# A linear-attention layer with a Hadamard FFN on one core: 32-wide corner tiles in the inverse, the FFN weight fold moved into the setup, clearings moved ahead, and new step orders

## What is computed

```
qkvz = xn @ w_qkvz.T ;  q, k, v, z per head        (32 heads of 64)
q, k, v = causal conv over 4 tokens, per channel
g = -exp(A_log) * softplus(a + dt_bias) ; beta = sigmoid(b)
q, k = l2norm(q) / 8, l2norm(k)
for t:  S = S * exp(g_t) ; delta = (v_t - k_t S) * beta_t
        S = S + k_t^T delta ; o_t = q_t S
attention = (rmsnorm(o) * norm_weight * sigmoid(z)) @ w_out.T

u = fwht(xn * SU_ug) ; h = silu(u W_gate) * (u W_up)      (1024 wide)
ffn = (fwht(h * SU_dp) @ W_down.T) * Wscale_dp
```

## Time and profile before

| | us |
|---|---|
| median of 3 runs | 921.9 (918.11 to 922.74) |
| the profiled execution, its own time | 921.86 |
| its span | 920.0 |
| TensorE busy | 845.0 (92%) |
| VectorE busy | 703.3 (76%) |
| GpSimd busy | 287.7 (31%) |
| ScalarE busy | 256.0 (28%) |

### The profile page before, as it was taken

The page is one execution under the profiler, slowest core; times in us unless marked ns, Lnnn a source line. Parts: engine busy times, 40 slices in busy tenths (PEclk is TensorE's granted clock), DMA queues, the critical chain, the costliest instruction groups (busy, mean ns, idle before and its releaser), DMA issues.

```text
span 920.0 us, 30578 instructions
## 1 busy us (share of the span) xinstructions
PE 845.0 (92%) x13354; PEld 607.2 (66%) x13354; DVE 703.3 (76%) x1248; ACT 256.0 (28%) x560; POOL 287.7 (31%) x194
## 2 busy tenths in 40 slices
PE   1887499999999999999999999999999999998685
PEld 1533267766767676767676677767777767767574
DVE  5675968888887979788887878797978888795522
ACT  2333114132332314141423223241414132331000
POOL 2019531514124242324142322423231513233110
PEclk9989699999999999999999999999999999999877
DMA  4323031131413131413213141304131231210101
GB/s 124 128 58 81 6 77 36 31 82 30 94 30 83 23 80 37 69 32 64 60 31 82 30 94 24 89 19 77 42 58 44 41 84 30 60 31 14 30 2 46
DMA packets 129157, 49.56 MB, mean 54 GB/s; under 512 B 110977, under 2 KB 120449, under 8 KB 128897
## 3 DMA queue, kind: packets, MB, share of 16 engines
q1 hardware_dynamic: 129024, 47.62, 23.8%
HBM read 39.98 MB, written 7.60 MB: 52 GB/s over the span
## 4 chain that ended last, share of the span: by engine, by line
PE 60%; DVE 17%; SPq 7%; DMA 6%; POOL 5%; issue 3%; ACT 1%; POOLq 0%; DVEq 0%; ACTq 0%
PE bank L581 17%; DVE kq L224 4%; PE bank L645 4%; PE bank L593 3%; PE bank L747 3%; SPq L512 3%; PE bank L662 3%; PE bank L749 3%; PE bank L692 3%; PE bank L602 3%; PE bank L664 3%; PE bank L730 2%; PE bank L668 2%; PE bank L719 2%; PE bank L678 2%
## 5 line engine op out<-in xcount | busy, mean ns | idle before, releaser
L581 PE MATMUL bank<-xnT,wq 128*128 128x512 f32 x512 | 261.8, 636 | 15.8 <-DVE kq L224 15.5
L224 DVE SCALAR_TENSOR_TENSOR kq<-bank,cw,kq 128x510 f32<-128x510 f32 (+2 forms) x288 | 214.6, 745 | 44.9 <-ACT kq L798 37.8
L581 PEld LDWEIGHTS bank<-xnT,wq 128*128 128x128 f32 x512 | 90.7, 195 | 98.1 <-issue 70.3
L948 POOL TENSOR_TENSOR ost<-ost,cst 128x8 f32<-128x8 f32 x32 | 52.3, 1634 | 191.7 <-DVE ost L357 191.7
L798 ACT ACTIVATE kq<-bank,cw 128x512 f32<-128x512 f32 x96 | 65.8, 685 | 143.3 <-PE bank L581 142.5
L944 POOL TENSOR_TENSOR Sd<-St,dec 128x256 f32<-128x256 f32 x32 | 19.9, 621 | 231.7 <-DVE St L345 161.4
L938 POOL TENSOR_TENSOR kqg<-kq,rows 128x1024 f32<-128x1024 f32 x32 | 75.5, 2358 | 39.0 <-DVE kq L224 39.0
L645 PE MATMUL bank<-kq 64*64 64x128 f32 x1024 | 69.0, 274 | 11.6 <-DVE kq L224 8.9
L911 POOL TENSOR_TENSOR kd<-kc,stat 128x512 f32<-128x512 f32 x32 | 33.4, 1042 | 144.1 <-DVE stat L261 144.1
L747 PE MATMUL bank<-wo,oT 128*128 128x256 f32 x256 | 70.6, 389 | 1.6 <-DVE oT L369 1.6
L270 DVE TENSOR_TENSOR ATP<-bank,gb 128x512 f32<-128x512 f32 x64 | 44.1, 689 | 30.4 <-issue 14.3
(11 more groups left out here) (132 smaller groups left out, 1449.1 us busy)
## 6 DMA issues: line engine op xcount, KB each, us to landing
rows<-decay_rows SPq DMA_DIRECT2D x64, 256.0 KB, 4.6
wq<-wqkvz_dram SPq DMA_DIRECT2D x16, 512.0 KB, 3.7
inverse_blocks<-UU SPq DMA_DIRECT2D x16, 256.0 KB, 2.0
woraw<-wout_dram SPq DMA_DIRECT2D x16, 128.0 KB, 2.2
wguT<-wgu_dram SPq DMA_DIRECT2D x8, 256.0 KB, 5.2
base_blocks<-ATP SPq DMA_DIRECT2D x128, 16.0 KB, 2.7
NT<-base_blocks SPq DMA_DIRECT2D x16, 128.0 KB, 2.1
U<-inverse_blocks SPq DMA_DIRECT2D x128, 16.0 KB, 2.0
```

The lines of the kernel that those rows point to most:

```text
L224: nc.vector.scalar_tensor_tensor(out=y[:, :, t:S], in0=p[:, :, 0:S - t], scalar=cw[:, m, i // 2, 3 - t:4 - t], in1=y[:, :, t:S], op0=ALU.m ...
L581: last = nc.tensor.matmul(ring[i % 2][:], wq[:, q, kc, i // 2, :], xnT[:, kc, (i % 2) * 512:(i % 2) * 512 + 512], start=kc == 0, stop=kc = ...
L948: nc.gpsimd.tensor_tensor(ost[:, 2, :], ost[:, 1, :], k("neghalf")[:, 0:B * 2], ALU.pow).then_inc(rms_done, 1)
```

## The change

- **Corner tiles.** hz.1 on TensorE is cut from one 64 x 64 corner for a head to the two 32 x 32 corners on its diagonal (twice the matmuls, 48 columns each). hz.3 loads only the 32 left columns of Q and writes the top 32 rows.
- **Fold in the setup.** `fold` is gone from GpSimd. W_down is loaded early into the memory of `kqg` (`wds`); VectorE multiplies it by wsd (two halves) and does six butterflies of 128 x 1024 in the setup; TensorE's 128-wide part then waits for them, and ScalarE's copy takes in the scale. The two multiplications stand around `var` (L395), one butterfly ahead of each of VectorE's two copies of xnT, four behind `coef`. GpSimd's first `kqg.0` waits for `wd_ready`.
- **Clearings first.** The four memsets stand ahead of the layernorm's power.
- **DMAs.** wsd, ah (4) and nwh (2) are issued by ScalarE ahead of its first squares; SyncE's wait for xnT is gone.
- **Orders.** All five lists are new. They are turned round (other letters), and apart from that these steps move. TensorE: ktr.1 from behind ks.3 to between proj.4 and ks.3; gram.0 from ahead of proj.4 to behind ks.3; proj.6 from ahead of vtr.0 to ahead of proj.7; qsq from ahead of delta.1 to behind it, proj.2 ahead of delta.1. VectorE: vtr.0 from behind gram.1 to behind hz.3.1; inv.1 from behind ks.2 to behind state.1; proj.2 behind ks.2; out.0 ahead of proj.5. ScalarE: qsq, qsum, dec, delta.3 and oload move, inv.2 ahead of proj.5. GpSimd: kd.0 from ahead of gb.0 to behind kqg.1, kd.1 from ahead of sd.2 to behind it, kqg.0 ahead of norm.1. SyncE: load from behind bin to ahead of bout, oload between bout and bin, fload behind uout.

```diff
@@ vector, setup
+                def butterfly(src, dst, h, t):
+                    s4, d4 = (w.rearrange("p (a t h) d -> p a t h d", t=2, h=h) for w in (src, dst))
+                    step(nc.vector.tensor_tensor(d4[:, :, t], s4[:, :, 0], s4[:, :, 1], (ALU.add, ALU.subtract)[t]))
+                def wscaled(i):
+                    step(nc.vector.tensor_tensor(wds[1][:, 4 * i:4 * i + 4], wds[0][:, 4 * i:4 * i + 4], wsd[:].unsqueeze(1).broadcast_to([P, 4, HID]), ALU.mult))
+                dve.wait_ge(wdn_in, 16)
+                dve.wait_ge(wsd_in, 16)
+                wscaled(0)
                 dve.wait_ge(sq_done, TT)
                 step(nc.vector.tensor_scalar(st[:, 0, :], st[:, 2, :], 1.0 / HID, LN_EPS, ALU.mult, ALU.add))
                 steps["var"] = count[0]
+                wscaled(1)
...
                 for q in (1, 3):
+                    butterfly(wds[1], wds[0], 1, q // 2)
                     dve.wait_ge(xnT_ready, q + 1)
...
+                for t in range(2):
+                    butterfly(wds[0], wds[1], 2, t)
+                for t in range(2):
+                    butterfly(wds[1], wds[0], 4, t)
+                steps["fold"] = count[0]
@@ vector, list
-K.out.0 K.turn.1 K.out.1 M.e M.stats K.out.2 K.out.3 M.gram.0 L.hz.0.0 L.hz.0.1 M.gram.1 M.vtr.0 L.hz.1.0 L.hz.1.1
-M.gram.2 L.hz.2.0 L.hz.2.1 M.ff M.gram.3 L.hz.3.0 L.hz.3.1 A.proj.0 L.state.0 M.vtr.1 L.ks.1 A.proj.1 M.inv.0 L.state.1
-A.proj.2 L.ks.2 M.inv.1 L.norm.0 L.state.2 A.proj.3 L.ks.3 L.gated.0 M.inv.2 L.turn.0 L.norm.1 A.proj.4 L.gated.1
-A.proj.5
+A.proj.5 L.turn.1 L.out.1 A.e A.stats L.out.2 L.out.3 A.gram.0 M.hz.0.0 M.hz.0.1 A.gram.1 M.hz.1.0 M.hz.1.1 A.gram.2
+M.hz.2.0 M.hz.2.1 A.ff A.gram.3 M.hz.3.0 M.hz.3.1 A.vtr.0 P.proj.0 M.state.0 A.vtr.1 M.ks.1 P.proj.1 A.inv.0 M.state.1
+A.inv.1 M.ks.2 P.proj.2 M.norm.0 M.state.2 P.proj.3 M.ks.3 M.gated.0 A.inv.2 M.turn.0 M.norm.1 P.proj.4 M.gated.1
+M.out.0
@@ sync
+                sp.dma_start(wds[0], wdown).then_inc(wdn_in, 16)
-                sp.wait_ge(xnT_ready, 4)
-                sp.dma_start(wdT[:], wdown).then_inc(wdn_in, 16)
-M.rload M.fload L.bout L.bin A.load L.uout L.uin L.oload
+L.rload M.load K.bout K.oload K.bin K.uout L.fload K.uin
@@ tensor, hz
+                        if j == 1:
+                            for rs, cs in ((top, slice(0, H2)), (low, slice(H2, C))):
+                                for h in range(2):
+                                    last = nc.tensor.matmul(M[H][rs[h], i * n:i * n + n], Q[rs[h], u, cs], U16[rs[h], u, C - n:C], start=True, stop=True)
+                            continue
...
-                                last = nc.tensor.matmul(M[H][hs[h], i * n + n - H2:i * n + n], Q[hs[h], u, :], X[hs[h], q, u, H2:C], start=True, stop=True)
+                                last = nc.tensor.matmul(M[H][top[h], i * n + n - H2:i * n + n], Q[hs[h], u, 0:H2], X[hs[h], q, u, H2:C], start=True, stop=True)
@@ tensor, list
-M.proj.4 K.ks.3 M.ktr.1 K.delta.3 K.turn.0 K.o.1 M.proj.5 K.out.0 K.out.1 M.proj.6 M.vtr.0 K.turn.1 M.proj.7 K.out.2
-K.out.3 M.ff L.hz.0.0 L.hz.0.1 M.gram.1 L.hz.1.0 L.hz.1.1 M.gram.2 L.hz.2.0 L.hz.2.1 M.gram.3 L.hz.3.0 L.hz.3.1
-A.proj.0 L.delta.0 M.vtr.1 L.state.0 A.proj.1 L.ks.1 M.qsq L.delta.1 A.proj.2 L.state.1 L.o.0 L.ks.2 A.proj.3 L.delta.2
-A.ktr.0 L.state.2 A.gram.0
+K.hz.2.0 K.hz.2.1 L.gram.3 K.hz.3.0 K.hz.3.1 M.proj.0 K.delta.0 L.vtr.1 K.state.0 M.proj.1 K.ks.1 M.proj.2 K.delta.1
+L.qsq K.state.1 K.o.0 K.ks.2 M.proj.3 K.delta.2 M.ktr.0 K.state.2 M.proj.4 M.ktr.1 K.ks.3 M.gram.0 K.delta.3 K.turn.0
+K.o.1 M.proj.5 K.out.0 K.out.1 M.vtr.0 K.turn.1 M.proj.6 M.proj.7 K.out.2 K.out.3 M.ff L.hz.0.0 L.hz.0.1 M.gram.1
+L.hz.1.0 L.hz.1.1 M.gram.2
@@ scalar, list
-A.ktr.0 L.delta.3 A.proj.4 A.ktr.1 L.norm.1 A.proj.5 M.inv.2 A.proj.6 A.proj.7 A.ff A.qsq P.proj.0 M.delta.0 P.proj.1
-M.oload M.delta.1 A.qsum P.proj.2 M.norm.0 M.delta.2 P.proj.3 P.dec
+K.oload L.proj.7 L.ff M.proj.0 K.delta.0 M.proj.1 L.qsq K.delta.1 M.proj.2 L.qsum K.norm.0 K.delta.2 M.proj.3 M.ktr.0
+M.proj.4 K.delta.3 M.ktr.1 K.norm.1 L.inv.2 M.proj.5 M.proj.6 M.dec
@@ gpsimd
-                    if m == 0 and H == 1:
-                        fold()
+                        if m == 0:
+                            pool.wait_ge(wd_ready, 4)
...
-P.kqg.0 P.kd.0 P.gb.0 P.root P.gb.1 P.kqg.1 A.sd.1 P.kd.1 A.sd.2 A.norm.0 A.norm.1
+K.norm.1 M.gb.0 M.root M.gb.1 M.kqg.1 M.kd.0 L.sd.1 L.sd.2 M.kd.1 L.norm.0 A.kqg.0
```

More of the change, by code:

```diff
@@ L152, in layer @@
         su, sd_, wsu, wsg = (vec[:, a:a + n] for a, n in ((0, KC), (KC, IT), (KC + IT, IT), (KC + 2 * IT, IT)))
-        wdT = xs
+        wds = [kqg[:, i].rearrange("p k u c -> p (k u c)").rearrange("p (i d) -> p i d", i=IT) for i in range(2)]
         names = """w_in row_in wo_in nw_in ff_in at_out nb_in uu_out ui_in proj_done tap0_done conv_step z_done E_done
@@ L662, in hz @@
                                 last = nc.tensor.matmul(dst, ATP[hs[h], q, u, 0, :], T16[hs[h], u, 0:n], start=True, stop=True)
-                            elif j == 1:
-                                last = nc.tensor.matmul(dst, Q[hs[h], u, :], U16[hs[h], u, C - n:C], start=True, stop=True)
                             elif j == 2:
@@ L773, in _ @@
                     last.then_inc(xh_ready, 1)
-                pe.wait_ge(wdn_in, 16)
+                pe.wait_ge(v_step, steps["fold"])
                 for m in range(4):
                     pe.wait_ge(xh_done, m + 1)
-                    nc.tensor.matmul(spare[m][:], k("had"), wdT[:, 2 * m:2 * m + 2, :], start=True, stop=True).then_inc(wd_ready, 1)
+                    nc.tensor.matmul(spare[m][:], k("had"), wds[0][:, 2 * m:2 * m + 2, :], start=True, stop=True).then_inc(wd_ready, 1)
                 program({"proj": proj, "ff": ff, "ktr": ktr, "vtr": vtr, "qsq": qsq, "gram": gram, "hz": hz, "ks": ks, "delta": delta,
-                         "state": state, "o": o, "turn": turn, "out": out}, """M.proj.4 K.ks.3 M.ktr.1 K.delta.3 K.turn.0 K.o.1 M.proj.5 K.out.0 K.out.1 M.proj.6 M.vtr.0 K.turn.1 M.proj.7 K.out.2
-                         K.out.3 M.ff L.hz.0.0 L.hz.0.1 M.gram.1 L.hz.1.0 L.hz.1.1 M.gram.2 L.hz.2.0 L.hz.2.1 M.gram.3 L.hz.3.0 L.hz.3.1
-                         A.proj.0 L.delta.0 M.vtr.1 L.state.0 A.proj.1 L.ks.1 M.qsq L.delta.1 A.proj.2 L.state.1 L.o.0 L.ks.2 A.proj.3 L.delta.2
-                         A.ktr.0 L.state.2 A.gram.0""")
+                         "state": state, "o": o, "turn": turn, "out": out}, """K.hz.2.0 K.hz.2.1 L.gram.3 K.hz.3.0 K.hz.3.1 M.proj.0 K.delta.0 L.vtr.1 K.state.0 M.proj.1 K.ks.1 M.proj.2 K.delta.1
+                         L.qsq K.state.1 K.o.0 K.ks.2 M.proj.3 K.delta.2 M.ktr.0 K.state.2 M.proj.4 M.ktr.1 K.ks.3 M.gram.0 K.delta.3 K.turn.0
+                         K.o.1 M.proj.5 K.out.0 K.out.1 M.vtr.0 K.turn.1 M.proj.6 M.proj.7 K.out.2 K.out.3 M.ff L.hz.0.0 L.hz.0.1 M.gram.1
+                         L.hz.1.0 L.hz.1.1 M.gram.2""")
             @block.scalar
@@ L856, in oload @@
                     nc.scalar.activation(wo[:, q], woraw[:], ACT.Copy, scale=nwh[:]).then_inc(wo_done, 1)
+                act.dma_start(wsd[:], ws_dp.broadcast_to([P, HID])).then_inc(wsd_in, 16)
+                for h in range(2):
+                    for m, src in enumerate((alog, dtb)):
+                        act.dma_start(ah[hs[h], m, :], src[h:h + 1, :].broadcast_to([C, PAIRS])).then_inc(gate_in, 16)
+                for h in range(2):
+                    act.dma_start(nwh[hs[h], :], nw).then_inc(nw_in, 16)
                 for t in range(TT):
```

49 lines of the change are left out of this document (15 added, 34 removed).

## The result

The changed kernel takes 955.9 us (median of four, 950.4 to 960.0) against 920.9 for the kernel before on the same chip: the ratio is 1.038, 95% interval 1.032 to 1.044. It is slower by 35 us, where 909 was forecast. Its profiled execution took 950.4 us, span 948.6. Two of the ten executions of the changed kernel with hz.1 64 wide (experiment 1) took 1067 us at a mean clock of 0.75 and count in no ratio; its profile is of one of them and still has 10.4 us of idle time that no semaphore ends, so whether such stops are gone is read from experiments 2 and 8.

A forecast was written before the change was run, and what follows sets the result against it. TensorE was taken to bound the loop at 50.21 us a pair. From 921.9 us, the head's 15.0 came off and 14 pairs at +0.18 added 2.5, giving 909; 8 in 10 for 892 to 921.

The forecast's parts named there:

- Corner tiles: TensorE's hz.1 and hz.3: hz.1 +0.28 us, the gram behind it +0.13, hz.3 -0.77; together -0.36 us a pair.
- C: Rival, slower than before: hz.1's 128 small records keep the 64-wide pace of 0.029 us; 936 us, chance 0.06.
- B: Rival, no new waits: GpSimd's ops slip into gaps of inv.1, or the delay is absorbed; 895 us, chance 0.30.
- D: Rival, head and loop at their bad ends: W_down late, NT late, 1.8 us of waits a pair; 922 us, chance 0.16.
- Fold: First pair: VectorE's products no longer stall beside GpSimd's fold; gain 12.5 us, bounds 9 to 13.
- Setup: Before the first pair: clearings gain 4.0 us, less 0.5, 1.2 and 0.8 for added work; net gain 1.5, bounds -1 to 3.5.
- a sign of its being wrong: Setup: the prediction is wrong if the first xnT is no earlier than the 17.9 us it has now.
- The head as a whole: Up to hz.0 of pair 0: fold 12.5, kd.0 1.0 and setup 1.5; gain 15.0 us, bounds 10 to 18.
- VectorE's order: Loop: inv.1's products, now beside GpSimd's sd.2 and kd.1, are locked out 1.35 us; TensorE waits 1.15 us more a pair.
- the work of VectorE from state.1 to ks.3 is the same as before: Loop, VectorE: unchanged work leaves only 0.2 us of slack, so 1.15 us a pair come back as TensorE's waits.
- TensorE's and SyncE's order: Loop: one run of 128-wide work less, -0.33 us a pair, and 0.28 us of idle time gone.

The follow-up runs named there:

- experiment 1: The changed kernel with hz.1 again as 64 products of 64x64, hz.3 still half as wide; 914.5 us, ratio 0.994 of the kernel before.
- experiment 2: The changed kernel with both corner products, hz.1 and hz.3, 64x64 as before the change; 918.9 us, ratio 1.000 of the kernel before.
- experiment 8: The changed kernel with all five engines' old lists and hz.1 64 wide, keeping new setup, fold and narrow hz.3; 899.2 us, ratio 0.980.
- experiment 7: The changed kernel with hz.1 computing the upper corner only, 64 products of 32x32 instead of 128; 909.4 us, ratio 0.992 of the kernel before.
- experiment 11: VectorE's new list alone, added to the kernel with new setup and fold, narrow hz.3, 64-wide hz.1 and old lists; 915.5 us, ratio 0.993.

## Why the prediction was wrong

The ratios of the runs make a ladder from the kernel before to the changed one, each step one part (the intervals are about 0.3% each, so no step is better than 0.4%; each ratio is against the kernel before on the same chip, but the chips differ from step to step):

| step | ratio from, to | share | forecast |
|---|---|---|---|
| setup and fold | 1, 0.991 | -0.9%, -8 us | -15 us |
| hz.3 narrow | 0.991, 0.980 | -1.1%, -10 us | -0.77 x 14 = -11 |
| VectorE's list | 0.980, 0.993 | +1.3%, +12 us | +1.15 x 14 = +16 |
| GpSimd's list | 0.993, 0.999 | +0.6%, +5 us | in the line above |
| TensorE's, ScalarE's, SyncE's lists | 0.999, 0.994 | -0.5%, -5 us | (-0.33 - 0.28) x 14 = -9 |
| hz.1 in corners | 0.994, 1.038 | +4.4%, +41 us | +0.41 x 14 = +6 |

The steps depend on their order: between experiments 2 and 1, with the new lists, the narrow hz.3 is worth 0.7%, not 1.1.

**The step that failed** is "Corner tiles", and in it the price of hz.1. I priced the records by how fast TensorE runs them, with bounds from 0.010 to 0.029 us a record, and never asked whether something has to bring them. By that price the term was wrong on the good side: 11.6 ns were measured where 15.6 were forecast, so hz.1 became 0.36 us shorter, not 0.28 longer. The 41 us are in the main stops outside hz.1, in hz.2 and hz.3 (32 us more of them than without the corner tiles, experiment 2), which were on no line of the sum. Its source was wrong as well: hz.2's 32 columns stood for hz.1's 48, since "the moving columns don't set the time", but two corners with 48 columns took 23 ns a record in experiment 7 where hz.2 takes 17.7, and only the four corners in turn brought it down to 11.6. The forecast should have bounded it from the rows of before: the page's row of the instruction queue (105 packets, 1.72 MB), 16.4 KB or 256 instructions a block, and the chain, by which hz.1 would have become 128 matmuls and 128 weight loads, a whole block, in about 2 us. A resource that takes part in the new stretch and has no row at that load had to get a rival of its own.

The Trainium skill has the mechanism (Runtime: NRT & Kernel Launch, section Instruction fetch mechanics): instructions come in 16 KiB blocks of 256 through a DMA queue of the sequencer's own, while the engine executes. The trace agrees with the block: 16.4 KB a packet, 254 instructions from restart to restart. The same section says that this fetch is hidden because instructions are issued more slowly than they are filled in; here the trace shows otherwise, 33.5 us of stops in 948.6. By that rule the tiles would have cost nothing, and by the block of 256 it names they deserved the question.

**The rivals.** C forecast 936, slower through hz.1, for the reason that its records would keep the pace of the wide ones, 29 ns. The sign is right, the mechanism isn't: they run at 11.6. B (no new waits) and D (late W_down, late NT) didn't decide. The 25 ns of the Trainium skill (TensorE: Matmul & The Clock Gate, section Wait — 56ns, not 53.3ns?) are far above the 11.6 ns of hz.1.

**Fold: right.** The four products of the earlier trace rows are at their usual durations in the changed kernel (the second and third take 0.17 each):

```profile
87.65 0.43 DVE L296 TENSOR_TENSOR UU<-NT,cst 128x256 f32<-128x256 f32 x1 [5.24 <-DMA NT<-base_blocks]
...
89.08 0.57 DVE L306 TENSOR_TENSOR prod<-UU 128x64 f32<-128x64 f32 x2
```

From the arrival of NT to the blocks' going out it is 100.95 - 87.65 = 13.3 us, where it was 113.79 - 88.08 = 25.7: 12.4 gained, 12.5 forecast.

**Setup: wrong in sign.** -1.5 was forecast. The eight normalisations took 2.7 us (from the clearings -4, right), but x landed 2.3 us later through ScalarE's loads, priced at 0 to 0.8 for their issue only and not for what they do to another queue's landing; W_down held VectorE for 3.62 us until 13.7; and the power took 2.61 us instead of 1.64 beside wscaled(1):

```profile
15.19 1.23 DVE L401 TENSOR_TENSOR kqg<-kqg,wsd 128x1024 f32<-128x1024 f32 x1
...
15.31 2.61 POOL L965 TENSOR_TENSOR st<-st,cst 128x8 f32<-128x8 f32 x1 [9.85 <-DVE st L407]
```

That last one was forecast (0 to 1.2, I took 1.2; it is 1.0): the exclusion works both ways. The first transpose came at 19.55 instead of 17.95, which the prediction had named as a sign of its being wrong. By the landing of NT, 87.65 instead of 88.08, setup and kd.0 had brought only 0.4 of the 2.5 us forecast. The gate matmuls took 3.94 us instead of 7.04, for a reason that the traces don't show (the granted clock is given as 1.00 in both); in the run of setup and fold alone they take 6.98, and NT is there at 89.11, later than before the change. The head as a whole still gained 12.9 us of the 15.0; with the old lists, in the run of setup and fold alone, hz.0 starts at 116.3, 9.7 earlier, and 1.5 us of that is lost again by the last pair (45.7 us against 44.1), which I can't explain.

**VectorE's order: right in size, half wrong in kind.** +1.15 a pair was forecast; the two lists measured +17 us, 1.2 a pair. But the way there was another, and that the sizes meet is in part luck: the stall in inv.1 is 0.35 + 0.41 = 0.76 us a pair (L306 0.91, L310 0.98 for 0.56 and 0.57), not 1.35; another 0.53 a pair stands in norm's L357 (13.8 us for 5.3 over 16 pairs), which I didn't have. And most of the cost stands without it: with VectorE's list alone, where L310 isn't stalled, 12 of the 17 us are there. I put that down to the step "the work of VectorE from state.1 to ks.3 is the same as before": the sum is the same, but proj.2's conv moved from the front of it to the back. Waits of TensorE for it account for 3.1 us of those 12 (experiment 11); the rest isn't shown.

**TensorE's and SyncE's order: right in sign, half the size.** The 0.5%, with ScalarE's list in them, are just beyond the intervals of two runs on different chips; no run has these lists alone.

## What to carry to other kernels

Splitting a matmul into smaller tiles is paid for in instructions, and these arrive at a limited rate: count the instructions of a stretch against the time that it lasts (here TensorE stopped where two blocks of 256 in a row lasted 2.6 and 3.1 us, and hardly where the first lasted 3.0), and look for idle time with no semaphore whose place drifts from one turn of a loop to the next. Large data transfers in the same microseconds make it worse. In an order of work, price each step by what waits behind it, not by the sum of the stretch.
